# Attention weighing of two key blocks at a time, in a fused attention and expert kernel

## The reference, cut to what matters

```
q = xt @ Wq.T                      # 512 x 256, split into 8 heads of 32
scores = scale * einsum('bhqd,bhkd->bhqk', qh, qh)
attn = softmax((scores * cmask + (1 - cmask) * NEG) * rmask)
ctx = einsum('bhqk,bhkd->bhqd', attn, qh)
out = ctx @ Wo.T
```

## Time and profile before

| what | value |
|---|---|
| median of 3 runs | 1361.45 us (1361.18 to 1362.42) |
| the profiled execution | 1362.26 us, span of the profile 1360.5 us |
| mean granted PE clock over the span | 0.933 of 2.4 GHz |
| PE / DVE / ACT / POOL busy | 92% / 50% / 38% / 51% of the span |
| attention bodies of rows 1 to 14 | from 82.61 us to 646.24 us |

### The profile page before, as it was taken

The page is one execution under the profiler, slowest core; times in us unless marked ns, Lnnn a source line. Parts: engine busy times, 40 slices in busy tenths (PEclk is TensorE's granted clock), DMA queues, the critical chain, the costliest instruction groups (busy, mean ns, idle before and its releaser), DMA issues. The chain is left out here.

```text
span 1360.5 us, 21962 instructions
## 1 busy us (share of the span) xinstructions
PE 1252.7 (92%) x5564; PEld 689.3 (51%) x5565; DVE 686.2 (50%) x1178; ACT 523.7 (38%) x992; POOL 696.4 (51%) x602
## 2 busy tenths in 40 slices
PE   4999999999999999999932599999999999989998
PEld 2444454444544544544312344444444444479997
DVE  3677666676666667666349322222222222226666
ACT  1365555555555655555610122222222222212221
POOL 1387777687787777777835422222222222035443
PEclk7699899899999999999965699999999999989999
DMA  6555635445645544544045142222222222248787
GB/s 179 144 142 149 165 116 149 123 125 142 164 120 145 155 117 125 157 133 111 17 182 205 39 124 87 87 89 93 93 93 93 86 86 90 69 161 286 265 280 229
DMA packets 93921, 184.06 MB, mean 135 GB/s; under 512 B 11408, under 2 KB 13968, under 8 KB 93888
## 3 DMA queue, kind: packets, MB, share of 16 engines
q1 hardware_dynamic: 83008, 148.00, 37.3%
q0 software_dynamic: 10880, 35.66, 8.4%
HBM read 130.60 MB, written 52.49 MB: 135 GB/s over the span
## 5 line engine op out<-in xcount | busy, mean ns | idle before, releaser
L664 DVE TENSOR_REDUCE row_max<-bank 128x1 f32<-128x512 f32 x512 | 335.9, 686 | 154.9 <-PE bank L498 148.6
L608 ACT ACTIVATE probsT<-bank 128x512 f32<-128x512 f32 x512 | 291.9, 597 | 243.0 <-PE bank L510 227.5
L387 POOL TENSOR_TENSOR key_sum<-key_sum,probsT 128x1024 f32<-128x1024 f32 x128 | 301.9, 2371 | 40.2 <-ACT probsT L608 40.2
L498 PE MATMUL bank<-k_stack,q_stack 96*128 96x512 f32 x512 | 270.0, 531 | 15.1 <-DVE row_max L664 12.3
L1192 PE MATMUL bank<-gate_up_sb,rows_T 128*128 x576 | 273.7, 598 | 1.6 <-ACT rows_T L1127 1.6
L383 POOL TENSOR_TENSOR key_sum<-probsT 128x1024 f32<-128x1024 f32 x64 | 151.6, 2378 | 123.2 <-ACT probsT L608 122.3
L510 PE MATMUL bank<-q_stack,k_stack 99*128 99x512 f32 x512 | 211.9, 415 | 0.9 <-ACT probsT L608 0.9
L498 PEld LDWEIGHTS bank<-k_stack,q_stack 96*128 96x128 f32 x512 | 102.2, 200 | 199.5 <-DVE row_max L664 128.9
L1192 PEld LDWEIGHTS bank<-gate_up_sb,rows_T 128*128 128x128 f32 x576 | 104.8, 192 | 106.7 <-issue 106.7
L520 PE MATMUL bank<-probsT,vals 128*32 128x512 f32 x1024 | 146.1, 644 | 0.7 <-ACT probsT L608 0.7
L1078 POOL COPY row_prob<-slot_prob 128x1 f32 (+1 forms) x72 | 13.2, 183 | 258.7 <-DVE rows_scaled L1093 255.6
(11 more groups left out here) (141 smaller groups left out, 1512.7 us busy)
## 6 DMA issues: line engine op xcount, KB each, us to landing
expert_rows_dram<-rows_out SPq DMA_DIRECT2D x72, 256.0 KB, 2.1
k_stack<-hi_dram SPq DMA_DIRECT2D x64, 256.0 KB, 4.0
q_stack<-hi_dram SPq DMA_DIRECT2D x64, 256.0 KB, 6.7
x_row<-in_x SPq DMA_DIRECT2D x16, 512.0 KB, 3.7
hi_dram<-q_hi SPq DMA_DIRECT2D x32, 256.0 KB, 2.0
lo_dram<-q_lo SPq DMA_DIRECT2D x32, 256.0 KB, 2.0
k_stack<-lo_dram SPq DMA_DIRECT2D x32, 256.0 KB, 4.9
q_stack<-lo_dram SPq DMA_DIRECT2D x32, 256.0 KB, 6.3
```

The source lines that it names most:

```text
L387: nc.gpsimd.tensor_tensor(total, total, probs(k), ALU.add).then_inc(added, 1)
L498: nc.tensor.matmul(logit_bank[i % 2][:, :], q_stack[par][g][0:K_LOGIT, h, q * P:(q + 1) * P], k_stack[par][g][0:K_LOGIT, h, :], start=True ...
L608: nc.scalar.activation(probsT[:, j, :], key_bank[j % 2][:, :], ACT.Exp, scale=SCALE).then_inc(probs_ready, 1)
L664: nc.vector.tensor_reduce(row_max[g][:, i:i + 1], logit_bank[i % 2][:, :], AX.X, ALU.max)\
```

## The change

`weigh` is no longer called after each key block (slots with j = 5, 9 and 13 for k = 0, 1 and 2, and j = 1 of the next unit for k = 3). It is called twice in a row: for k = 0 and 1 in the slots with j = 9, and for k = 2 and 3 in the slots with j = 1 of the next unit. The number of products is the same.

```diff
--- before.py
+++ after.py
@@ -546,16 +546,16 @@
                         find_logits(*place(b, par, g, du + 1), i)
                     find_keys(b, par, g, j)
                     use_misc(b, kind, s)
-                    if j % HPU == 1:
-                        if j > HPU:
-                            weigh(b, g, j // HPU - 1)
-                        elif g == 1:
-                            weigh(b, 0, NQ - 1)
-                        elif kind != FIRST:
-                            weigh(b - 1, 1, NQ - 1)
+                    if j == 2 * HPU + 1:
+                        for k in range(2):
+                            weigh(b, g, k)
+                    if j == 1 and (g == 1 or kind != FIRST):
+                        for k in range(2, NQ):
+                            weigh(b if g == 1 else b - 1, 1 - g, k)
 
             rows(pe, body)
-            weigh(B - 1, 1, NQ - 1)
+            for k in range(2, NQ):
+                weigh(B - 1, 1, k)
             use("tail_sums1", tail("tail_sums1"), add_up, B - 1, 1)
             for e in range(2):
                 use(f"tail_hid{e}", tail(f"tail_hid{e}"), hidden_half, B - 1, e)
```

## The result

| | before | changed |
|---|---|---|
| median | 1361.32 us (4 runs, 1358.45 to 1362.42) | 1393.04 us (4 runs, 1387.69 to 1397.48) |
| the profiled execution | 1362.26 us | 1395.95 us |
| its span | 1360.5 us | 1394.2 us |
| its mean granted clock | 0.933 | 0.918 |
| body of rows 1 to 14, mean | 40.26 us | 42.27 us |

The changed kernel is slower: the ratio is 1.0235, 95% interval 1.019 to 1.0279. Of its four runs the two shorter ones (1387.7 and 1390.1 us) had a mean granted clock of 0.925 and 0.924, the two longer ones (1396.0 and 1397.5) 0.918, so part of its spread is clock.

What follows compares the result with a forecast made beforehand. PE was taken as the bound on average, with runs of bare slots going at DVE's pace. Profiled 1362.3 us plus 17 at full clock plus 7 for clock dips gave about 1386 us, range 1371 to 1398.

Steps and rivals of the forecast that it cites:

- A block behind a block: Slots 1, 9, 17 and 25: a second quarter-width block costs 0.85 us, four more a body, +3.40 us.
- Slot 5: Block taken out: slots 5 and 6 go from 2.13 to 1.28 us as bare slots, saving 0.85 us.
- Slot 21: Block taken out: its whole 1.21 us goes, but slot 22 slows from 0.46 to about 0.64; saved 1.0 us.
- Slots 13 and 29: Blocks taken out: PE waits for DVE's row maxima instead, so only 0.2 us saved each, not 1.21.
- Full clock: One attention body of 32 slots at full clock: the terms sum to +1.15 us, 16.1 for 14 bodies.
- The waits: PE's wait for DVE's row maxima becomes longer and more frequent; its weight load waited 8.4 us in 14 pieces before.
- The clock: Emptied slot 29 before the router: a dip in nearly every body, 14 in place of 9, 5 x 1.4 = +7 us.
- The case of more clock lost: Rival: a dip in each body at slot 30 plus about half at slot 13, or some long; 1396 us, chance 0.15.
- The rest: Outside the 14 full bodies: rows 0 and 15 together come to +0.5 to +1 us.
- The sum: Whole kernel: 1362.3 + 17 at full clock + 7 for clock dips = 1386.3, about 1386 us; chance 0.5.
- the switch is what counts: Rival: halving the weighing's quarter-to-full-width switches saves 0.36 us each, four a body; faster, 1340 us, chance 0.07.
- The clock as before: Rival: slower, but with nine clock dips again; 1362 + 17 = 1379 us, chance 0.24.

Runs made afterwards that it cites:

- e7: The changed kernel with DVE's normalisation of the even unit moved from slot 27 to slot 30: 1373.9 us, ratio 1.011 to the kernel before.
- e1: Against the kernel before, only key blocks 0 and 1 are weighed together (slots 9 and 25), 2 and 3 stay: 1354.1 us, ratio 0.9946.
- e5: Against the kernel before, key block 1 is weighed in slot 12 in place of slot 9, the others stay: 1349.2 us, ratio 0.9937.
- e6: Against the kernel before, key block 1 joins key block 2 in slots 13 and 29, the others stay: 1360.9 us, ratio 1.0012.
- e4_keep13: The changed kernel with key block 2 of group 0 left in slot 13: 1374.2 us, ratio 1.0119 to the kernel before.

## Why the prediction was right, and where its sizes were off

The forecast was 1386 us, 1371 to 1398; measured 1393.04. The sign and the mechanism held; the size is a little off: a ratio of 1.018 forecast, just below the 1.019 to 1.0279 measured. (I had taken 2.7 us as the least difference that runs can tell; that interval is 6 us to either side.)

- *A block behind a block*, 0.85 us, four more in a body: measured 0.85 in slot 9 and 0.86 in slot 17.
- *Slot 5*, saved 0.85: measured 2.13 - 1.29 = 0.84. *Slot 21*, saved 1.0: measured 1.2 (472.57 - 470.47 = 2.10 before, 324.95 - 324.04 = 0.91 changed), since slot 22 did not slow down.
- *Slots 13 and 29*, saved 0.2 each: measured 0.22 and about 0.13. This was the term on which the sign hung, and e7 shows its cause in slot 29 by moving it.
- *Full clock*, forecast +1.15 a body, measured 1.0 (1.05 in the pair with the smaller router): 14 us for 14 bodies, forecast 16.
- *The waits.* PE's own wait for the row maxima grew as forecast, from 0.7 to 2.1 us in a body. The weight load's did not: it fell from 8.4 to 5.7 us, in fewer pieces.
- *The clock* is the term that was mis-sized. I had 14 dips in place of nine, at 1.4 us each: +7. Their number came out, but not their length: seven bodies take 41.4 to 41.8 us, three 44.5 and three 42.1 to 42.3; in the first, at 40.20, the clock falls only a microsecond before its end. By a full-clock body of 40.1 the short dips cost 1.3 to 1.7 and the longest 4.4: the clock took 14 us more in these bodies. The case of more clock lost, 0.15 in my chances, had two forms: long dips, which came, and a second dip at slots 11 to 14, which did not come in any body.
- *The rest.* For rows 0 and 15 together I had +0.5 to +1, for the later stages nothing. Row 1 begins 1.1 us later, and behind row 14 it is 4.5 more: 1.9 of these up to the last copy of the router's logits (L761, at 697.30 before and 728.43 changed), 2.6 in the stages behind it, which the change does not touch. Their cause was not tested.
- *The sum.* By the profiled executions it is 14 + 14 + 1.1 + 4.5 = 33.7 us, against 17 + 7 = 24 forecast. The clock took twice what I gave it; the total still fell into the range because the range reached up to a case of more clock lost, and part of that case was one that did not come.

Of the rivals: *the switch is what counts* is not what ruled this change, but its price is real. In e1, where the emptied slots hide no long wait, the joinings bring a gain, 39.07 to 38.7 us a body: of the 2 x 0.36 = 0.72 us that two joinings save, the waits that open take about half. The rule on tiling modes in the Trainium skill (TensorEngine Tiling (Array Packing), Key Properties: a change of mode drains the TensorE) agrees with e1 and with the 0.36 us a block. Yet e5, with two more quarter-width stretches in a body, is faster than the kernel before. *The clock as before* (1379) fell with the 14 dips. That long quarter-width runs cost in themselves fell with e6 and e1.

What stays open: why some dips are longer than others, and why the time at 1.2 GHz grows most where slots 13 and 29 are both emptied.

## What to carry to other kernels

A piece of work that an engine does just before it would have to wait is nearly free there: here 0.13 to 0.22 us of a block's 1.21. Before moving it to save a switch, find what ends last in the slot that it leaves. Here the same joining gained 0.5% out of slots 5 and 21 and lost 2.6% out of slots 13 and 29, and a move towards the waits gained 1.5%. And work taken out of a thin stretch of TensorE can be paid for a second time, in clock.

## What the runs showed that I had not expected

In e4_keep13 and e7_late_norm, both with a full-clock body of 39.4 to 39.5 us by their slots, 12 of the 14 bodies of rows 1 to 14 take 40.92 to 41.02 us, each with one short dip. The two differ in their work in slots 13, 17 and 29, by about 0.07 us a body at full clock, and yet the 12 bodies of rows 2 to 13 take 491.59 us in both (121.67 to 613.26 and 123.92 to 615.51). So a few hundredths of a microsecond at full clock brought nothing while a dip stayed in each body; whether this holds for a few tenths was not tested. The four runs of e7 vary little (1372.7 to 1374.7 us), those of e4 more (1372.7 to 1379.6), and more still those of kernels in which dips come and go (e1: 1349.1 to 1358.0, e6: 1356.7 to 1367.6).
